# Second cross layer: the transposes of the probabilities two steps behind their scores, with a third buffer

## The reference

```python
q = rms_norm((x @ wq).reshape(B, L, 16, 128), q_norm_w)
k = rms_norm((x @ wk).reshape(B, L, 4, 128), k_norm_w)        # v without the norm
k_ctx = rms_norm((h_ctx_kv @ wk_ctx)..., k_norm_w)            # v_ctx = h_ctx_kv @ wv_ctx
q = q * cos + rotate_half(q) * sin ; k = k * cos + rotate_half(k) * sin
scores = einsum('blhd,bmhd->bhlm', q, [k_ctx, k]) / sqrt(128) + mask   # causal on k, open on k_ctx
out = einsum('bhlm,bmhd->blhd', softmax(scores), [v_ctx, v]).reshape(B, L, 2048) @ wo
```

## Time and profile before

| | us |
|---|---|
| median of 3 runs | 1594.97 |
| the three runs | 1594.99, 1588.06, 1594.97 |
| profiled execution: its time | 1592.06 |
| profiled execution: its span | 1589.6 |
| PE busy | 1409.4 (89% of the span) |
| DVE busy | 987.5 (62%) |
| ACT busy | 730.8 (46%) |
| POOL busy | 433.1 (27%) |

### The profile page before, as it was taken

The page is one execution under the profiler, slowest core; times in us unless marked ns, Lnnn a source line. Parts: engine busy times, 40 slices in busy tenths (PEclk is TensorE's granted clock), DMA queues, the critical chain, the costliest instruction groups (busy, mean ns, idle before and its releaser), DMA issues.

```text
span 1589.6 us, 25738 instructions
## 1 busy us (share of the span) xinstructions
PE 1409.4 (89%) x9822; PEld 887.5 (56%) x9840; DVE 987.5 (62%) x1782; ACT 730.8 (46%) x1747; POOL 433.1 (27%) x385
## 2 busy tenths in 40 slices
PE   7869999998899789999999988988975888988888
PEld 3535555554466456665666854755652545555636
DVE  6784323224588567777775876937778676674641
ACT  3452111112777455655664546358756453352230
POOL 3230000000000387777770000110291135224100
PEclk9979999998999989999999989999997889988899
DMA  7020311003000300000001000020010100000000
GB/s 247 27 80 1 93 31 31 0 0 159 1 2 2 120 7 7 8 7 7 8 1 74 1 22 0 1 79 2 2 45 25 54 1 2 2 1 2 28 0 27
DMA packets 21804, 48.10 MB, mean 30 GB/s; under 512 B 1458, under 2 KB 16947, under 8 KB 20532
## 3 DMA queue, kind: packets, MB, share of 16 engines
q1 hardware_dynamic: 21684, 46.47, 8.4%
HBM read 41.22 MB, written 5.24 MB: 29 GB/s over the span
## 4 chain that ended last, share of the span: by engine, by line
PE 59%; DVE 21%; ACT 7%; POOL 7%; issue 5%; DMA 0%; DVEq 0%; ACTq 0%; POOLq 0%
PE PS L748 43%; PE PS L962 5%; DVE work L2299 5%; PE PS L827 3%; PE PS L1269 2%; PE PS L1023 2%; DVE small L1849 2%; ACT work L1540 2%; PE PS L760 2%; POOL WB L621 1%; POOL WB L620 1%; POOL work L627 1%; POOL work L624 1%; PE PS L1298 1%; DVE work L1994 1%
## 5 line engine op out<-in xcount | busy, mean ns | idle before, releaser
L748 PE MATMUL PS<-XT,WB 128*128 128x512 f32 (+1 forms) x688 | 301.9, 601 | 8.6 <-issue 5.4
L748 PEld LDWEIGHTS PS<-XT,WB 128*128 128x128 f32 (+1 forms) x688 | 127.2, 192 | 153.0 <-issue 150.8
L1540 ACT ACTIVATE work<-PS,small 128x128 f32<-128x128 f32 x512 | 138.0, 419 | 48.2 <-DVE small L2099 48.2
L2069 DVE TENSOR_TENSOR work<-PS,work 128x512 f32<-128x512 f32 x48 | 33.1, 691 | 168.0 <-PE PS L748 168.0
L571 POOL TENSOR_SCALAR small<-small 128x4 f32<-128x4 f32 x22 | 5.0, 229 | 423.9 <-DVE small L1852 423.9
L1496 ACT ACTIVATE work<-PS 128x512 f32<-128x512 f32 x48 | 28.7, 597 | 193.6 <-PE PS L748 193.6
L2099 DVE TENSOR_REDUCE small<-PS 128x4 f32<-128x512 f32 x128 | 80.6, 684 | 44.2 <-PE PS L748 44.0
L748 PE MATMUL PS<-XT,WA 128*128 128x512 f32 (+2 forms) x224 | 101.4, 630 | 6.9 <-ACT XT L1403 3.3
L2299 DVE SCALAR_TENSOR_TENSOR work<-PS,vec,work 128x508 f32<-128x508 f32 (+2 forms) x108 | 80.2, 742 | 17.9 <-ACT work L1667 8.6
L962 PE MATMUL PS<-WB,work 128*128 128x256 f32 x384 | 86.6, 379 | 0.0
L748 PE MATMUL PS<-WA,XT 128*128 128x256 f32 (+1 forms) x384 | 79.9, 368 | 3.8 <-DVE XT L2119 3.0
(11 more groups left out here) (365 smaller groups left out, 2951.5 us busy)
## 6 DMA issues: line engine op xcount, KB each, us to landing
WB<-in_l0f SPq DMA_DIRECT2D x8, 768.0 KB, 7.7
WB<-in_l1x SPq DMA_DIRECT2D x1, 6144.0 KB, 17.5
WB<-in_l0f SPq DMA_DIRECT2D x32, 96.0 KB, 7.2
WB<-in_l2f SPq DMA_DIRECT2D x1, 3072.0 KB, 10.5
WA<-in_l3a SPq DMA_DIRECT2D x1, 2624.0 KB, 9.0
WB<-in_l3f SPq DMA_DIRECT2D x1, 2064.0 KB, 7.6
WA<-in_l1f SPq DMA_DIRECT2D x1, 2056.0 KB, 11.3
C<-in_ctx SPq DMA_DIRECT2D x2, 1024.0 KB, 7.1
```

What stands on the lines that cost most here:

```text
L748: mm = lambda o, l, r, s, e: nc.tensor.matmul(o, l, r, start=s, stop=e)
L1540: f(wk(12288 + (u % 8) * G + h * P, P), bank(j)[:, h * P:(h + 1) * P], ACT.Exp, bias=sm(704 + (u % 8) * 4 + h, 1)).then_inc(*act_step(*([j ...
L2069: v.tensor_tensor(l0f_h(m)[:, lo:lo + G], bank(j), l0f_s(m)[:, lo:lo + G], ALU.mult).then_inc(*dve_step(j))
```

## The change

The transposes of the probabilities move from one step behind the scores to two, the value product from two to three, the output product from three to four, on PE, in the list of the banks, and in what ACT and DVE take out. The loops get one step more at their end. Since probabilities live a step longer, `l1x_p` has three buffers in turn in place of two; the third lies in WB, columns 7168 to 8192, where the value weights of the context were. The waits that guard the buffers follow: ACT's exponentials of step t wait for the transposes of t - 3 in place of t - 2, and at t = 2, the first use of the third buffer, for the weights' transfer.

```diff
--- before.py
+++ after.py
@@ -86,7 +86,7 @@
 
 
     l = list(ln)
-    for t in range(-4, 35):
+    for t in range(-4, 36):
         w, r = t // 4 + 1, t % 4
         if 0 <= t < 32:
             l += [("s", t, 0), ("s", t, 1)]
@@ -94,12 +94,12 @@
             l += [[("k", w), ("q", w, 0), ("q", w, 1)], [("k2", w), ("q", w, 2), ("q", w, 3)], [("rq", w)], []][r]
             if w % 4 == 0:
                 l += [("v", w // 4, r)]
-        if 1 <= t < 33:
-            l += [("t", t - 1, 0), ("t", t - 1, 1)]
         if 2 <= t < 34:
-            l += [("pv", t - 2)]
-        if 3 <= t:
-            l += [("o", t - 3)]
+            l += [("t", t - 2, 0), ("t", t - 2, 1)]
+        if 3 <= t < 35:
+            l += [("pv", t - 3)]
+        if 4 <= t:
+            l += [("o", t - 4)]
         if w < 8 and r == 2:
             l += [("rt", w)]
     p["l1x"] = l
@@ -449,7 +449,7 @@
 
         def l1x_p(u):
 
-            return wk(16384, 1024) if u % 2 == 0 else XN[:, 0:1024]
+            return (wk(16384, 1024), XN[:, 0:1024], WB[:, 7168:8192])[u % 3]
 
         def l1x_pt(u):
 
@@ -1052,8 +1052,8 @@
                         for c in range(2):
                             ins = mm(o, xt(c, b * P, (b + 1) * P), wx("v", c * G, c * G + G), c == 0, c == 1)
                         end(ins)
-                if 1 <= t < 33:
-                    x = t - 1
+                if 2 <= t < 34:
+                    x = t - 2
                     pe.wait_ge(dve_to_pe.sem, dve_to_pe.next())
                     for kc in range(2):
                         o = begin("l1x", "t", x, kc)
@@ -1061,8 +1061,8 @@
                             ins = nc.tensor.transpose(o[:, j * P:(j + 1) * P],
                                                       l1x_p(x)[:, j * D + kc * P:j * D + (kc + 1) * P], cst("ident"))
                         end(ins)
-                if 2 <= t < 34:
-                    x = t - 2
+                if 3 <= t < 35:
+                    x = t - 3
                     g, kv, b = x // 16, x // 4 % 4, x % 4
                     o = begin("l1x", "pv", x)
                     if kv == 0:
@@ -1072,8 +1072,8 @@
                         pe.wait_ge(*freed(J("l1x", "t", x, kc)))
                         ins = mm(o, l1x_v(g, b, kc)[:, kv * P:(kv + 1) * P], l1x_pt(x)[:, kc * G:(kc + 1) * G], kc == 0, kc == 1)
                     end(ins)
-                if 3 <= t:
-                    x = t - 3
+                if 4 <= t:
+                    x = t - 4
                     o = begin("l1x", "o", x)
                     pe.wait_ge(*freed(J("l1x", "pv", x)))
                     for hh in range(4):
@@ -1575,14 +1575,16 @@
 
 
             ln("l1x")
-            for t in range(-4, 34):
+            for t in range(-4, 35):
                 w, r = t // 4 + 1, t % 4
                 if 0 <= t < 32:
                     for s_ in range(2):
                         j = J("l1x", "s", t, s_)
                         act.wait_ge(dve_to_act.sem, dve_to_act.next())
-                        if s_ == 0 and t >= 2:
-                            act.wait_ge(*full(J("l1x", "t", t - 2, 1)))
+                        if s_ == 0 and t == 2:
+                            act.wait_ge(wb_in, 16)
+                        if s_ == 0 and t >= 3:
+                            act.wait_ge(*full(J("l1x", "t", t - 3, 1)))
                         for i in range(2):
                             q = 2 * s_ + i
                             f(l1x_p(t)[:, q * D:(q + 1) * D], bank(j)[:, i * D:(i + 1) * D], ACT.Exp,
@@ -1625,15 +1627,15 @@
                         j = J("l1x", "v", w // 4, r)
                         act.wait_ge(*full(j))
                         f(l1x_v(w // 4, r, 1), bank(j), ACT.Copy).then_inc(*act_step(j))
-                if 1 <= t < 33:
-                    x = t - 1
+                if 2 <= t < 34:
+                    x = t - 2
                     j = J("l1x", "t", x, 1)
                     act.wait_ge(*full(j))
                     if x >= 2:
                         act.wait_ge(*full(J("l1x", "pv", x - 2)))
                     f(l1x_pt(x)[:, G:2 * G], bank(j), ACT.Copy).then_inc(*act_step(j))
-                if 2 <= t:
-                    x = t - 2
+                if 3 <= t:
+                    x = t - 3
                     j = J("l1x", "pv", x)
                     act.wait_ge(*full(j))
                     if x >= 3:
@@ -2201,11 +2203,11 @@
                 dve.wait_ge(key_normed.sem, key_normed.next())
                 v.reciprocal(l1x_root, l1x_root).then_inc(*dve_step(*([key_rooted] if w else [])))
 
-            for t in range(-3, 36):
+            for t in range(-3, 37):
                 w, r = (t - 1) // 4 + 1, (t - 1) % 4
                 base = 704 + (t % 4) * 16
-                if 4 <= t:
-                    x = t - 4
+                if 5 <= t:
+                    x = t - 5
                     b = 4 * (x // 16) + x % 4
                     j = J("l1x", "o", x)
                     dve.wait_ge(*full(j))
```

## The result

The changed kernel takes 1599.17 us (median of 17 runs, 1595.21 to 1605.4), the kernel before 1594.97 (17 runs, 1587.52 to 1602.1). The ratio is 1.0033 with a 95% interval of 1.0018 to 1.0048, which is +5.3 us (+2.9 to +7.7). The forecast was 1596 (1588 to 1603) and "within 0.5%".

A forecast was written before the change was run, and what follows sets the result against it. Regular windows were taken as bound by a loop of PE's scores, DVE and POOL, not PE's waits. Terms +2.4 - 0.3 = +2.1 us on 1592.06 gave 1594.2, 1597.1 by the median; 1596 was taken between, range 1588 to 1603.

The forecast's parts named there:

- The wait for the scalings, seven places: PE's 8.3 us of transposes waiting for DVE's scalings: the second four still wait for DVE's copy to free their bank; gain 0.
- The first window: Steps 0 to 3: PE idles some 4.1 us before step 4, the clock falls behind it; +2.4 us, within 1.7 to 2.9.
- 24 us and more: Sign of the clock fall: step 6's scores come this far behind those of step 4, against 21.99 before the change.
- The last window: Step 28's transposes lose their 1.91 us wait, but its value product still needs DVE's copy; -0.3 us.
- The rest: Third buffer, looser ACT wait and DVE's statistics moved one step on: together 0, within 0.7 us either way.
- A: Rival: the waits really go and the stage moves up by all 8.3 us, 1583.8 or 1586.7; chance 0.08.
- B: Rival: the wait turns into one for POOL, the clock holds; only the last window's -0.3, 1591.8 or 1594.7; chance 0.24.
- C: Rival: DVE's chain falls one 1.35 us POOL gap behind in six windows; +10.5 - 0.3, 1602.3 or 1605.2; chance 0.08.

The follow-up runs named there:

- e3: The changed kernel, but ACT copies the first half of the transposes and DVE the second; 1599.82 us, ratio 1.0033 to the kernel before.
- e11: The changed kernel with DVE's copy of the transposes moved ahead of the scalings in most steps, reciprocal left behind them; 1596.68 us, ratio 1.0006 to the kernel before.
- e7: The changed kernel with DVE's copy (most steps) and the key norm's reciprocal both moved ahead of the scalings; 1593.77 us, ratio 0.9991 to the kernel before.
- e1: The changed kernel with step 0's value product computed three times to keep PE busy ahead of step 4; 1597.31 us, ratio 1.0009 to the kernel before.
- e2: The changed kernel, but transposes of steps 0 to 2 stay one step behind, two from step 3 on; 1597.18 us, ratio 1.003 to the kernel before.
- e5: The changed kernel, but transposes of steps 0 to 11 stay one step behind, two from step 12 on; 1596.75 us, ratio 1.0011 to the kernel before.
- e4: The kernel before, with transposes two steps behind only from step 27 on; 1596.94 us, ratio 1.0013 to the kernel before.
- e8: The kernel before, with three second-half value projections moved from steps 12, 13, 14 to 2, 3, 7; 1590.0 us, ratio 0.9969 to the kernel before.
- e10: The kernel before, with three second-half value projections moved into the first window, at steps 2, 3 and 3; 1589.97 us, ratio 0.9951 to the kernel before.
- e9: The changed kernel with DVE's copy and reciprocal ahead of the scalings, four value projections at steps 2, 2, 3, 3; 1589.0 us, ratio 0.996 to the kernel before.
- e6: The kernel before, with DVE's copy of the transposes moved ahead of the scalings in most steps; 1596.33 us, ratio 1.0003 to the kernel before.

## Why the prediction was right, and where it failed

*The wait for the scalings, seven places: 0.* Right, with its mechanism: the wait moved to the second four transposes, for the copy behind the scalings; windows 3 and 7 stay at 37.85 to 37.88, and e3 shows that what PE waits there is slack. The list of waits grew from 8.3 to 9.6 us while the windows stood still, and e3 and e11 move that time between three places of PE at nearly the same period (37.88, 38.03): a wait's length says nothing of its worth. One reading was off: PE's own work in a window was put at 36.66 and the most that could be gained at 1.19. It is 36.11 by window 7 of e7, so the most was 1.7: two rows that follow each other overlap by 0.17, so the idle times in the brackets are that much short, and the transposes at 624.72 hide 0.22.

*The first window: +2.4.* Measured +2.70, within 1.7 to 2.9. The idle time was 3.90 (4.1 was said), the clock fell behind it, and e1 and e2 each take the whole 2.7 away, one by work and one by order. But 1.7 to 2.9 was said of the scores of step 6, and these came 1.7 late, 23.68 behind those of step 4 where "24 us and more" was the sign; the other 1.0 came in on DVE beside POOL. The mechanism is right, and that 2.4 lies so near is in part luck.

*The last window: -0.3.* **This is the step that failed; it measured +4.16.** The prediction said that no instruction is added, that "the output products beyond the last scores only grow by one step's share while the part before shrinks by it". That is true of work and false of time. The small piece that was worked out holds: the value product of step 28 starts 4.72 behind the scores for 4.96, 0.24 sooner for the 0.3, and waits 1.45 for the copy. What shrinks is the first window, whose 36.1 us are set by POOL: taking 4.3 us out of it gave idle time (36.06 for 36.10). What grows is the tail, where PE is busy nearly without a break, and there each us of work is a us. The term should have been +4.32 for one step's three groups, less what the wait of 1.91 gives back. The rows for it stood in the timeline of PE; I worked out where the work of step 28 started and not how much of it came behind it. e7 shows the term bare: it has the deeper pipeline, its tail has no wait but the last, and it takes 40.86. The tail before without its wait of 1.91 and the 0.22 that goes with it (0.17 of overlap, 0.05 in the transposes) is 36.54, which is 4.32 less. e5 puts it to the test from the other side: the same work taken out of a window that PE sets gives 2.5 back. e4 shows that growing the lag at the last window doesn't avoid the cost.

*The rest: 0.* Right as a sum: one pair of statistics on DVE moved from window 5 to window 6, and the windows changed by -0.63 and +0.62. In e4, where the lag grows behind them, both are as before (38.72, 38.15).

*The rivals.* A (the waits really go and the stage moves up) is out by the stage, 6.80 longer, and by e3, B (the clock holds) by window 2, C (one gap of the comb in each window) by windows 3, 4 and 7. The case that happened, right in the windows and a step's work at the end, was not among them. That the time fell inside the range and within 0.5% all the same is no merit of the sum: the range was made wide by the spread of the runs and by room for C, and a miss of 4.5 us is only 0.3% of the time.

With the missing 4.32 put in, the last window is 4.32 - 0.3 = +4.0 and the sum +2.4 + 4.0 = +6.4, against +6.80 in the stage and +5.3 (2.9 to 7.7) by the ratio.

## What to carry to other kernels

Making a software pipeline one step deeper adds no instruction, and still moves one step's work from the fill to the drain: price the two ends apart, each by the engine that sets it. A wait is only worth removing if nothing in order behind the same event (a bank, a copy, a norm) comes at the same time; list these before the change, and move them with it, as e7 had to. The largest gain over the kernel before from a single idea (e8 and e10, 3.8 and 3.7 us of stage; 5.9 in e9 together with e7) came from looking for the window with no idle time and carrying its movable work to one that has some.

## What the runs showed of the hardware

- The granted clock fell behind idle times of 3.90 us (after), 2.59 (e4), 2.56 (e2), 2.24 (e6), 2.22 (e9) and once 1.91 (e10). It held behind the same 1.91 in the kernel before and in e8, and in the changed kernel it stood at 1.00 through an idle time of 3.21 (ahead of 583.22) and the work behind it. So in these runs the length of the idle time alone doesn't tell; what does stays open. PE lost 1.7 us at each of these falls, by the stretches at the lower level. In time such a fall cost nothing (e2), 1.7 (e10), 1.9 together with a longer wait (e6) or 2.70 (after), by where in its window it fell. The Trainium skill, in "TensorE: Matmul & The Clock Gate", section "HAM oscillation — how this bites in real kernels", puts the penalty at half of the throttled time; e10's tail agrees (1.7 worked out, 1.68 measured), and window 2 of the changed kernel shows that behind it the loss can grow (1.7 to 2.70).
- Work taken off DVE beside a busy POOL may save nothing (e6): four scalings that take 1.14 alone took 5.27 to 5.33 beside POOL's instructions, which start 1.35 apart, about one scaling for each.
